# One preln transformer block: the order of fill, projection and VectorE's products in steps 8 to 60

## The chip, the cores and the metric

The kernel runs on one core of one Trainium2 chip. Its time is the device time of one execution, in microseconds (us). The engines are PE (TensorE, matmuls), DVE (VectorE), ACT (ScalarE), POOL (GpSimd) and SP (SyncE, which issues DMA transfers). Each engine executes its own instructions in the order in which they are written, and waits for others by semaphores: an instruction that waits holds all that stands behind it on its engine.

## The reference

```python
x = x + attn(layernorm(x), wq, wk, wv, wo)      # x: 1024 x 256, 16 heads of 128
x = x + ffn(layernorm(x), w1, b1, w2, b2)       # 256 -> 1024 -> 256, exact gelu, ternary weights

def attn(h):
    q, k, v = heads(h @ wq), heads(h @ wk), heads(h @ wv)
    q, k = rotary(q), rotary(k)                 # x1*cos - x2*sin, x2*cos + x1*sin
    s = q @ k.T * 128**-0.5                     # only keys q-127 .. q are valid
    return concat(softmax(s) @ v) @ wo

def ternary(w):                                 # for w1 and w2
    scale = max(mean(abs(w)), 1e-8)
    return clip(round(w / scale), -1, 1)
```

## The kernel before, in words

The attention part is a software pipeline of 64 steps. A step n is one head and one quarter (256 rows) of the sequence: for n below 56, head n // 4 and quarter n % 4; the last eight steps, two heads, are taken in another order. A "chunk" m is half of the sequence of q or k of one head; there are 64 of them too, and a step computes chunk n + 4 ahead. fp32 products are made of three matmuls each, with operands split in a high and a low part (`_hi`, `_lo`).

What one step does, engine by engine, in steps 8 to 60 (`turned_first(n)` is true for these):

- PE: it transposes the probabilities of step n - 1 (`transpose_probs`, L488), computes the scores of step n (`scores`, L477), projects chunk n + 4 (`project`, L423, 512 columns each), then the "fill" (`fill`: either `project_v`, L442, a piece of v, or `project_out`, L459, a piece of the output product, twelve matmuls of 256 columns either way), then weighs v by the probabilities of step n - 1 (`weigh_v`, L505 to L508).
- DVE: it masks the transposed probabilities of step n - 1 (`mask_pt`, L873), selects the valid scores and takes their maximum (`merge`, L856 to L862), makes the low part of the head's output (`ot_lo`, L880), multiplies chunk n + 4 by the sine table (`times_sin`), takes the reciprocal of the row sums (`inverse_sum`, L867), multiplies the chunk by the cosine table (`times_cos`, both L825 or L827), and adds the output piece of the fill of step n - 1 to the residual (`add_out`, L886). In the even steps 34 to 48 one piece of the feed-forward weights is made ternary behind these (`ternary`, L904: two inputs in SBUF).
- ACT: `ot_hi` (L695), the exponentials (`exps`, L676), the copy of v if the fill of step n - 1 was one (`copy_v`, L690), the scaling of the probabilities by the reciprocal (`scale_probs`, L683), and the high part of the rotated chunk n + 3 (`rothi`, L671). Behind it, in some steps, stands the high part of a weight (L654, L660, L666), and in steps 18 to 25 a sum of absolute weights (L700).
- SP: the product by the sine table has its two halves swapped by two DMA transfers (`swap`, L306) as soon as it is there; weights are loaded behind it in the queue.
- POOL: the low part of chunk n + 2 (`rotlo`, L1088), the sum of the cosine product and the swapped sine product of chunk n + 3 (`rotate`, L1083), and, in some steps, the low part of a weight (L1070, L1074, L1078) or the first half of a ternary piece (`below`, L1095, odd steps 33 to 47).

So two chains run from step to step. The probabilities: scores, `merge`, `exps`, `inverse_sum`, `scale_probs`, and then PE's `transpose_probs(n)` at the head of step n + 1. The chunks: `project`, `times_sin`, the swap, `rotate`, `rothi`, `rotlo`, and then the scores of a later step.

"o step" below is a step on whose DVE list an `add_out` stands (n % 8 = 4 to 7); "v step" one on whose ACT list a `copy_v` stands (n % 8 = 0 to 3). Where n % 4 = 1, `weigh_v` has no L507 in it, since the first rows have no earlier keys.

Of the kernel before, what the change touches and what calls it, by code (L numbers as in the profile page):

```python
# [16 lines left out]
def preln_block_kernel(nc, x, wq, wk, wv, wo, w1t, b1, w2t, b2, cos_t, sin_t, in_prev, mask_t, ident, out):  # L17
# [13 lines left out]
    CHUNKS = 4 * HEADS  # L31
# [3 lines left out]
    with ExitStack() as ctx:  # L35
# [147 lines left out]
        LP = STEPS - 8  # L183
# [18 lines left out]
        def fills(n):  # L202

            if n >= LP:
                e = 4 * PAIRS
                return ((("v", e - 3),), (("v", e - 2),), (("v", e - 1),), (("o", e - 8),), (("o", e - 7),),
                        (("o", e - 4), ("o", e - 3)), (("o", e - 6),), (("o", e - 5),))[n - LP]
            if n < 2:
                return (("v", n + 2),)
            p, s = n // 8, n % 8  # L210
            if s == 7:
                return (("v", 4 * p + 4),)
            if s < 3:
                return (("v", 4 * p + s + 1),) if p > 0 else ()
            return (("o", 4 * p + s - 7),) if p > 0 else ()
# [19 lines left out]
        def turned_first(n):  # L235

            return 8 <= n < STEPS - 3
# [134 lines left out]
        def _(pe):  # L372
# [13 lines left out]
            def transpose_half(half):  # L386
                banks = xt_banks[half]
                if half == 0:
                    pe.wait_ge(cos_done, CHUNKS)
                else:  # L390
                    pe.wait_ge(pt_masked, STEPS)
                    pe.wait_ge(otlo_done, STEPS)
                for t in range(4):
                    pe.wait_ge(xn_ready, NT + half * 4 + t + 1)
                    for kd in range(KD):
                        tr = nc.tensor.transpose(banks[kd][:, t * P:(t + 1) * P],
                                                 xnorm[:, half * 4 + t, kd * P:(kd + 1) * P], ident_sb[:])
                        if t == 3:
                            tr.then_inc(xt_ready, 1)
# [11 lines left out]
            def project(m):  # L411
                head, c = chunk(m)
                a = head % 2
                if c == 0:
                    pe.wait_ge(qklo_done, head + 1)
                if m >= 2:
                    pe.wait_ge(cos_done, m - 1)
                if m in (0, 2):
                    pe.wait_ge(xt_lo_done, m + 2)
                n = 0  # L420
                for kd in range(KD):
                    for wt, xt in ((qk_lo[a], xT_hi), (qk_hi[a], xT_lo), (qk_hi[a], xT_hi)):
                        last = mm(PR[m % 2][:], wt[:, c % 2, kd], xt[:, kd, half_of(c)],  # L423
                                  start=(n == 0), stop=(n == 3 * KD - 1))
                        n += 1
                last.then_inc(proj_done, 1)
# [37 lines left out]
            def scores(n):  # L464
                head, j = step(n)
                if j % 2 == 0:
                    pe.wait_ge(rotlo_done, chunk_of[head, j + 1] + 1)
                if n >= 2:
                    pe.wait_ge(exp_done, 2 * n - 2)
                for i in range(2):  # L470
                    t = 2 * j + i
                    k0 = max(t - 1, 0)
                    o0 = i * 256 + (k0 - t + 1) * P
                    terms = ((rot_lo(head, 0), rot_hi(head, 1)), (rot_hi(head, 0), rot_lo(head, 1)),
                             (rot_hi(head, 0), rot_hi(head, 1)))
                    for p_, (q, k) in enumerate(terms):
                        last = mm(SC[n % 2][:, o0:(i + 1) * 256], q[:, t * P:(t + 1) * P], k[:, k0 * P:(t + 1) * P],  # L477
                                  start=(p_ == 0), stop=(p_ == 2))
                last.then_inc(scores_done, 1)

            def transpose_probs(n):
                pe.wait_ge(scaled, n + 1)
                if n > 0:
                    pe.wait_ge(pt_masked, n)
                if n == MEANS_AT:
                    pe.wait_ge(mean_read, 2)
                for i in range(2):
                    last = nc.tensor.transpose(PT[:, i * P:(i + 1) * P], probs[n % 2][:, i], ident_sb[:])  # L488
                last.then_inc(pt_done, 1)
# [20 lines left out]
            def means_of_abs():  # L510
                pe.wait_ge(abs_done, 8)
                pe.wait_ge(pt_masked, MEANS_AT - 1)
                mm(PT[:, 256:264], mean_ones[:], abs_sum[:].rearrange("p k i -> p (k i)"),
                   start=True, stop=True).then_inc(mean_done, 1)

            def fill(n):
                for kind, i in fills(n):
                    (project_v if kind == "v" else project_out)(i)
# [78 lines left out]
            for n in range(3, STEPS):  # L597
                if n == MEANS_AT:
                    means_of_abs()
                if turned_first(n):  # L600
                    transpose_probs(n - 1)
                scores(n)
                if not turned_first(n):
                    transpose_probs(n - 1)
                if n + 4 < CHUNKS:
                    project(n + 4)
                fill(n)
                if n == STEPS - 1:
                    transpose_half(0)
                weigh_v(n - 1)  # L610
# [173 lines left out]
        def _(dve):  # L784
# [30 lines left out]
            def xt_lo_half(half):  # L815
                hs = slice(half * HALF, (half + 1) * HALF)
                for kd in range(KD):
                    dve.wait_ge(xt_hi_done, 4 + half * 2 + kd + 1)
                    tt(xT_lo[:, kd, hs], xt_banks[half][kd][:], xT_hi[:, kd, hs].bitcast(F32),
                       ALU.subtract).then_inc(xt_lo_done, 1)  # L820
# [8 lines left out]
            def times_sin(m):  # L829
                dve.wait_ge(proj_done, m + 1)  # L830
                if m >= 2:
                    dve.wait_ge(rot_done, m - 1)
                times_table(by_sin[m % 2], m, sin_sb).then_inc(sin_done, 1)
# [31 lines left out]
            def inverse_sum(n):  # L865
                dve.wait_ge(exp_done, 2 * n + 2)
                nc.vector.reciprocal(rinv[:, n % 2], rowsum[:, n % 2]).then_inc(rinv_done, 1)  # L867
# [14 lines left out]
            def add_out(w):  # L882
                c = w % 4
                dve.wait_ge(wo_done, o_at[w] + 1)
                ts = slice(2 * c, 2 * c + 2)
                tt(xres[:, ts], VO[w % 2][:].rearrange("p (t d) -> p t d", t=2), xres[:, ts], ALU.add).then_inc(wo_added, 1)  # L886
# [95 lines left out]
            for n in range(3, STEPS):  # L982
                if n == STEPS - 2:
                    add_out(4 * PAIRS - 3)
                    tile_stats(1, 2)
                    tile_stats(1, 3)
                if n >= STEPS - 2:
                    ot_lo(n - 2)
                if n == STEPS - 1:
                    mask_pt(n - 1)  # L990
                if turned_first(n):
                    mask_pt(n - 1)
                if n == MEANS_AT:
                    mean_sums()
                merge(n)
                if not turned_first(n) and n < STEPS - 1:
                    mask_pt(n - 1)
                if n == STEPS - 2:
                    moments(3)
                if n < STEPS - 2:  # L1000
                    ot_lo(n - 2)
                if n + 4 < CHUNKS:
                    times_sin(n + 4)
                if n == STEPS - 1:
                    xt_lo_half(0)
                inverse_sum(n)
                if n == STEPS - 2:
                    add_out(4 * PAIRS - 6)
                    normalise(3)
                if n + 4 < CHUNKS:  # L1010
                    times_cos(n + 4)
                if n <= LP + 4:
                    for kind, w in fills(n - 1):
                        if kind == "o":
                            add_out(w)
                if n == LP + 4:
                    add_out(4 * PAIRS - 7)
                if n == STEPS - 3:
                    add_out(4 * PAIRS - 4)
                    tile_stats(1, 0)  # L1020
                    tile_stats(1, 1)
                if n == MEANS_AT:
                    thresholds()
                i = (n - BELOW_AT - 1) // 2
                if n > BELOW_AT and (n - BELOW_AT) % 2 == 1 and i < PIECES:
                    ternary(i)
# [145 lines left out]
```

## Time and profile before

| what | value |
|---|---|
| median of 3 runs | 346.85 us (346.25 to 346.94) |
| the profiled execution | 346.98 us, of it a span of 345.1 us |
| granted TensorE clock | 1.000 of full speed |
| PE busy | 335.9 us, 97% of the span |
| DVE busy | 272.0 us, 79% |
| POOL busy | 222.1 us, 64% |
| ACT busy | 208.0 us, 60% |
| chain that ended last | PE 85%, DVE 7%, POOL 2% |

Busy time is the union of an engine's instructions. Matmuls overlap in the pipeline, so the distance between two starts, and not the duration shown, is what one of them costs.

### The profile page before, as it was taken

What the parts mean: (1) busy time and instruction counts of PE and PEld (TensorE: products, weight loads), DVE (VectorE), ACT (ScalarE), POOL (GpSimd) and SP (SyncE); (2) the same over time, 40 slices, a digit from 0 to 9 for tenths busy, and PEclk for the clock granted to TensorE, in tenths of its full rate; (3) what the DMA queues carried; (4) which work ended last, traced back from release to release, by engine and by line L of the source; (5) the groups of instructions that cost most, each with busy time, mean ns of one, the idle gap of its engine ahead of it and who ended that gap; (6) DMA issues with size and microseconds to landing.
All of it is one profiled execution on the core that took longest, in us unless ns stands there. A gap on an engine that the chain in (4) does not pass through costs nothing.

```text
span 345.1 us, 6651 instructions
## 1 busy us (share of the span) xinstructions
PE 335.9 (97%) x2270; PEld 307.3 (89%) x2270; DVE 272.0 (79%) x608; ACT 208.0 (60%) x628; POOL 222.1 (64%) x181
## 2 busy tenths in 40 slices
PE   7997999999999999999999999999999999999996
PEld 6975789999999999999999999999999999988986
DVE  5889886778777886688789988898778777887782
ACT  3445766666677677655675566555775665567280
POOL 4326898765867586757899988898777567330400
DMA  7732563455554333333333333333322232000001
GB/s 222 188 109 62 140 167 92 123 142 146 141 147 94 84 91 93 92 92 80 78 84 81 83 89 92 93 92 93 91 64 56 49 83 60 0 3 0 32 30 61
DMA packets 29024, 31.23 MB, mean 90 GB/s; under 512 B 3392, under 2 KB 20288, under 8 KB 28992
## 3 DMA queue, kind: packets, MB, share of 16 engines
q1 hardware_dynamic: 28672, 30.29, 34.5%
q10 hardware_dynamic: 320, 0.52, 0.4%
q8 instruction: 18, 0.29, 0.4%
q14 instruction: 14, 0.11, 0.1%
HBM read 12.98 MB, written 1.05 MB: 41 GB/s over the span
## 4 chain that ended last, share of the span: by engine, by line
PE 85%; DVE 7%; POOL 2%; issue 2%; DMA 2%; ACT 1%; SPq 0%; DVEq 0%; POOLq 0%
PE PR L423 22%; PE VO L459 12%; PE VO L442 12%; PE SC L477 12%; PE OT L505 7%; PE PT L488 4%; PE OT L508 4%; PE OT L507 3%; PE VO L541 2%; PE PR L534 2%; PE SC L534 2%; PE SC L541 1%; POOL turn L1083 1%; DMA xres<-in_x 1%; DMA swapped<-by_sin 1%
## 5 line engine op out<-in xcount | busy, mean ns | idle before, releaser
L1088 POOL TENSOR_TENSOR gT_lo<-turn,gT_hi 128x512 fp32r<-128x512 f32 x61 | 80.6, 1322 | 40.9 <-ACT gT_hi L671 40.3
L1083 POOL TENSOR_TENSOR turn<-turn,swapped 128x512 f32<-128x512 f32 x61 | 78.9, 1293 | 30.7 <-DMA swapped<-by_sin 30.3
L676 ACT ACTIVATE probs<-SC,negmax 128x128 f32<-128x128 f32 x128 | 45.8, 363 | 68.6 <-DVE negmax L862 68.4
L873 DVE TENSOR_TENSOR probsT<-PT,mask_sb 128x512 f32<-128x512 f32 x64 | 44.1, 689 | 39.0 <-PE PT L488 38.8
L683 ACT ACTIVATE probs<-probs,rinv 128x128 f32<-128x128 f32 x128 | 44.4, 394 | 17.0 <-DVE rinv L867 17.0
L423 PE MATMUL PR<-xT_hi,qk_lo 128*128 128x512 f32 x128 | 50.5, 395 | 0.2 <-DVE xT_lo L812 0.2
L423 PE MATMUL PR<-xT_hi,qk_hi 128*128 128x512 f32 x128 | 50.6, 395 | 0.0
L423 PE MATMUL PR<-xT_lo,qk_hi 128*128 128x512 f32 x128 | 50.5, 394 | 0.0
L671 ACT CAST gT_hi<-turn 128x512 fp32r<-128x512 f32 x64 | 38.9, 608 | 10.8 <-POOL turn L1083 8.7
L477 PE MATMUL SC<-gT_hi,gT_lo 128*128 128x256 f32 (+1 forms) x128 | 41.3, 322 | 1.8 <-DVE gT_lo L848 1.8
L459 PE MATMUL VO<-o_lo,gT_hi 128*128 128x256 f32 x128 | 36.2, 283 | 0.3 <-DVE gT_lo L880 0.3
L505 PE MATMUL OT<-probsT,v_sb 128*128 128x256 f32 x120 | 36.0, 381 | 0.5 <-DVE gT_lo L880 0.4
L442 PE MATMUL VO<-v_lo,xT_hi 128*128 128x256 f32 x128 | 36.1, 282 | 0.0
L442 PE MATMUL VO<-v_hi,xT_hi 128*128 128x256 f32 x128 | 36.1, 282 | 0.0
L442 PE MATMUL VO<-v_hi,xT_lo 128*128 128x256 f32 x128 | 36.0, 281 | 0.0
L477 PE MATMUL SC<-gT_lo,gT_hi 128*128 128x256 f32 (+1 forms) x128 | 35.9, 281 | 0.0
L459 PE MATMUL VO<-o_hi,gT_hi 128*128 128x256 f32 x128 | 35.8, 280 | 0.0
L459 PE MATMUL VO<-o_hi,gT_lo 128*128 128x256 f32 x128 | 35.8, 280 | 0.0
L477 PE MATMUL SC<-gT_hi 128*128 128x256 f32 (+1 forms) x128 | 35.7, 279 | 0.0
L862 DVE TENSOR_REDUCE negmax<-SC 128x2 f32<-128x256 f32 x64 | 27.1, 424 | 2.2
L423 PEld LDWEIGHTS PR<-xT_hi,qk_hi 128*128 128x128 f32 x128 | 24.0, 187 | 5.1
L695 ACT CAST gT_hi<-OT 128x256 fp32r<-128x256 f32 x60 | 21.9, 365 | 9.8 <-PE OT L508 9.4
(126 smaller groups left out, 912.0 us busy)
## 6 DMA issues: line engine op xcount, KB each, us to landing
swapped<-by_sin SPq DMA_DIRECT2D x124, 128.0 KB, 2.3
v_raw<-in_wv SPq DMA_DIRECT2D x8, 256.0 KB, 2.9
qk_raw<-in_wq SPq DMA_DIRECT2D x16, 128.0 KB, 2.6
qk_raw<-in_wk SPq DMA_DIRECT2D x16, 128.0 KB, 2.8
o_raw<-in_wo SPq DMA_DIRECT2D x8, 256.0 KB, 3.0
xres<-in_x SPq DMA_DIRECT2D x4, 256.0 KB, 3.7
w_raw<-in_w1t SPq DMA_DIRECT2D x4, 256.0 KB, 3.4
w_raw<-in_w2t SPq DMA_DIRECT2D x4, 256.0 KB, 3.0
```

Of the source, the lines that this page charges most:

```text
L423: last = mm(PR[m % 2][:], wt[:, c % 2, kd], xt[:, kd, half_of(c)], start=(n == 0), stop=(n == 3 * KD - 1))
L442: last = mm(VO[v % 2][:, i * 256:(i + 1) * 256], xt[:, kd, t * P:(t + 1) * P], wt[:, kd], start=(n == 0), stop=(n == 3 * KD - 1))
L459: last = mm(VO[w % 2][:, i * 256:(i + 1) * 256], ot[:, t * P:(t + 1) * P], wt[:, a], start=(n == 0), stop=(n == 5))
L477: last = mm(SC[n % 2][:, o0:(i + 1) * 256], q[:, t * P:(t + 1) * P], k[:, k0 * P:(t + 1) * P], start=(p_ == 0), stop=(p_ == 2))
L505: mm(o[:, 0:2 * P], v_sb[:, t, hs], shared, start=True, stop=False)
L671: copy(rot_hi(head, c % 2)[:, half_of(c)], turn[m % 4][:]).then_inc(rothi_done, 1)
L676: nc.scalar.activation(probs[n % 2][:, i], SC[n % 2][:, i * 256 + P:(i + 1) * 256], ACT.Exp, bias=negmax[:, n % 2, i:i + 1], accum_out=row ...
L683: last = nc.scalar.activation(probs[n % 2][:, i], probs[n % 2][:, i], ACT.Copy, scale=rinv[:, n % 2, i:i + 1])
L862: nc.vector.tensor_reduce(negmax[:, n % 2], sc[:, :, 1], AX.X, ALU.max, negate=True).then_inc(negmax_done, 1)
L873: tt(probsT[:], PT[:, 0:256].rearrange("p (i q) -> p i q", i=2).unsqueeze(2).broadcast_to([P, 2, 2, P]), mask_sb[:].unsqueeze(1).broadcast ...
L1083: tt(turn[m % 4][:], turn[m % 4][:], swapped[m % 2][:], ALU.add).then_inc(rot_done, 1)
L1088: tt(rot_lo(head, c % 2)[:, half_of(c)], turn[m % 4][:], rot_hi(head, c % 2)[:, half_of(c)].bitcast(F32), ALU.subtract).then_inc(rotlo_don ...
```

## The change

In PE's list the fill of steps 8 to 59 stands ahead of the projection of chunk n + 4, and no longer behind it. In DVE's list of the same steps `times_sin` stands behind `inverse_sum`, and `add_out` of the previous step's fill ahead of both, and no longer behind `times_cos`. In step 60 there is no chunk left, so only DVE's `add_out` moves there. No instruction is added or removed, and the lists of ACT, POOL and SP stay as they are.

```diff
@@ tensor engine
-                if n + 4 < CHUNKS:
+                if turned_first(n) and n + 4 < CHUNKS:
+                    fill(n)
                     project(n + 4)
-                fill(n)
+                else:
+                    if n + 4 < CHUNKS:
+                        project(n + 4)
+                    fill(n)
@@ vector engine
-                if n + 4 < CHUNKS:
+                if n + 4 < CHUNKS and not turned_first(n):
                     times_sin(n + 4)
                 if n == STEPS - 1:
                     xt_lo_half(0)
+                if turned_first(n):
+                    for kind, w in fills(n - 1):
+                        if kind == "o":
+                            add_out(w)
                 inverse_sum(n)
+                if n + 4 < CHUNKS and turned_first(n):
+                    times_sin(n + 4)
...
                 if n + 4 < CHUNKS:
                     times_cos(n + 4)
-                if n <= LP + 4:
-                    for kind, w in fills(n - 1):
-                        if kind == "o":
-                            add_out(w)
```

On PE, step 37, from the last matmul of the scores (L477) on; L423 is the projection, L459 the fill, L505 to L508 `weigh_v`. Before:

```order
L477 MATMUL SC<-gT_hi 128x256
L423 MATMUL PR<-xT_hi,qk_lo 128x512
L423 MATMUL PR<-xT_lo,qk_hi 128x512
L423 MATMUL PR<-xT_hi,qk_hi 128x512
L423 MATMUL PR<-xT_hi,qk_lo 128x512
L423 MATMUL PR<-xT_lo,qk_hi 128x512
L423 MATMUL PR<-xT_hi,qk_hi 128x512
L459 MATMUL VO<-o_lo,gT_hi 128x256
L459 MATMUL VO<-o_hi,gT_lo 128x256
```

And now, the end of the same step, from the last matmuls of the fill on:

```order
L459 MATMUL VO<-o_hi,gT_lo 128x256
L459 MATMUL VO<-o_hi,gT_hi 128x256
L423 MATMUL PR<-xT_hi,qk_lo 128x512
L423 MATMUL PR<-xT_lo,qk_hi 128x512
L423 MATMUL PR<-xT_hi,qk_hi 128x512
L423 MATMUL PR<-xT_hi,qk_lo 128x512
L423 MATMUL PR<-xT_lo,qk_hi 128x512
L423 MATMUL PR<-xT_hi,qk_hi 128x512
L505 MATMUL OT<-probsT,v_sb 128x256
```

The projection moved from the place behind the scores to the place ahead of `weigh_v`; all else keeps its place.

On DVE, step 36 from `ot_lo` on, up to the mask of step 37's list. Line numbers behind the change are four higher. Before:

```order
L880 TENSOR_TENSOR gT_lo<-OT,gT_hi 128x256
L825 SCALAR_TENSOR_TENSOR by_sin0<-PR0,sin_sb 128x512
L867 RECIPROCAL rinv<-rowsum 128x2
L825 SCALAR_TENSOR_TENSOR turn0<-PR0,cos_sb 128x512
L886 TENSOR_TENSOR xres<-VO0,xres 128x512
L904 SCALAR_TENSOR_TENSOR w1_sb<-w1_raw,thr,w1_sb 128x512
L873 TENSOR_TENSOR probsT<-PT,mask_sb 128x512
```

And now:

```order
L884 TENSOR_TENSOR gT_lo<-OT,gT_hi 128x256
L890 TENSOR_TENSOR xres<-VO0,xres 128x512
L871 RECIPROCAL rinv<-rowsum 128x2
L829 SCALAR_TENSOR_TENSOR by_sin0<-PR0,sin_sb 128x512
L829 SCALAR_TENSOR_TENSOR turn0<-PR0,cos_sb 128x512
L908 SCALAR_TENSOR_TENSOR w1_sb<-w1_raw,thr,w1_sb 128x512
L877 TENSOR_TENSOR probsT<-PT,mask_sb 128x512
```

The two products by the tables stand next to each other behind the reciprocal, and the ternary piece stands right behind them, ahead of the mask.

## Rows read from the trace of the kernel before

**Rows 1.** Waits of PE, 45 to 300 us: engine, line, releaser, total us, times, longest.

```profile
PE VO L459 <- DVE gT_lo L880: 0.3, 1, 0.3
PE PT L488 <- ACT probs L683: 0.3, 1, 0.3
```

**Rows 2.** Timeline of PE, end of steps 37 and 41: start us, us, line, names, shapes.

```profile
187.26 0.28 PE L459 MATMUL VO<-o_lo,gT_hi 128*128 128x256 f32 x1
...
188.66 0.60 PE L505 MATMUL OT<-probsT,v_sb 128*128 128x256 f32 x2
...
189.32 0.38 PE L488 MATMUL PT<-ident_sb,probs 128*128 128x128 f32 x2
...
207.52 0.38 PE L488 MATMUL PT<-ident_sb,probs 128*128 128x128 f32 x2
```

**Rows 3.** Timeline of PE in a step that has L507.

```profile
157.11 0.38 PE L507 MATMUL OT<-probsT,v_sb 128*128 128x128 f32 x2
157.33 0.39 PE L508 MATMUL OT<-probsT,v_sb 128*128 128x128 f32 x2
```

**Rows 4.** Timeline of DVE, end of step 36 and start of 37.

```profile
182.85 0.69 DVE L825 SCALAR_TENSOR_TENSOR by_sin<-PR,sin_sb 128x512 f32<-128x512 f32 x1
183.46 0.15 DVE L867 RECIPROCAL rinv<-rowsum 128x2 f32<-128x2 f32 x1
183.53 0.67 DVE L825 SCALAR_TENSOR_TENSOR turn<-PR,cos_sb 128x512 f32<-128x512 f32 x1
184.12 0.68 DVE L886 TENSOR_TENSOR xres<-VO,xres 128x512 f32<-128x512 f32 x1
184.72 0.74 DVE L904 SCALAR_TENSOR_TENSOR w_sb<-w_raw,thr,w_sb 128x512 fp32r<-128x512 f32 x1
185.38 0.68 DVE L873 TENSOR_TENSOR probsT<-PT,mask_sb 128x512 f32<-128x512 f32 x1
...
186.88 0.41 DVE L880 TENSOR_TENSOR gT_lo<-OT,gT_hi 128x256 fp32r<-128x256 f32 x1
```

**Rows 5.** Timeline of ACT: scaling of step 36, first exponential of step 37 (o steps).

```profile
183.65 0.69 ACT L683 ACTIVATE probs<-probs,rinv 128x128 f32<-128x128 f32 x2 [0.38 <-DVE rinv L867]
...
187.00 0.37 ACT L676 ACTIVATE probs<-SC,negmax 128x128 f32<-128x128 f32 x1 [1.48 <-DVE negmax L862]
```

**Rows 6.** Timeline of ACT, step 41 (a v step).

```profile
205.19 0.37 ACT L676 ACTIVATE probs<-SC,negmax 128x128 f32<-128x128 f32 x1 [1.48 <-DVE negmax L862]
...
206.45 0.69 ACT L683 ACTIVATE probs<-probs,rinv 128x128 f32<-128x128 f32 x2
```

**Rows 7.** Timeline of DVE: the sine product of chunk 39, in step 35.

```profile
178.29 0.69 DVE L827 TENSOR_TENSOR by_sin<-PR,sin_sb 128x512 f32<-128x512 f32 x1 [0.17 <-PE PR L423]
```

**Rows 8.** Timeline of POOL, step 36: sum of chunk 39, a weight's low part.

```profile
181.94 1.30 POOL L1083 TENSOR_TENSOR turn<-turn,swapped 128x512 f32<-128x512 f32 x1 [0.27 <-DMA swapped<-by_sin]
183.19 1.29 POOL L1074 TENSOR_TENSOR v_lo<-v_raw,v_hi 128x512 fp32r<-128x512 f32 x1
```

**Rows 9.** Timeline of POOL, step 34: a weight's low part.

```profile
174.21 1.29 POOL L1070 TENSOR_TENSOR qk_lo<-qk_raw,qk_hi 128x512 fp32r<-128x512 f32 x1
```

**Rows 10.** Timeline of DVE, step 34: the first ternary piece.

```profile
174.95 1.10 DVE L904 SCALAR_TENSOR_TENSOR w_sb<-w_raw,thr,w_sb 128x512 fp32r<-128x512 f32 x1
```

**Rows 11.** Timeline of ACT, an early step in which PE waits for it.

```profile
29.88 0.69 ACT L683 ACTIVATE probs<-probs,rinv 128x128 f32<-128x128 f32 x2 [1.63 <-DVE rinv L867]
```

**Rows 12.** The same place on PE.

```profile
30.63 0.44 PE L488 MATMUL PT<-ident_sb,probs 128*128 128x128 f32 x2 [0.38 <-ACT probs L683]
```

**Rows 13.** DMA queues, 130.5 to 131.0 us: kind, packets, MB, share of 16 engines.

```profile
q8 instruction: 1, 0.02, 18.2%
```

**Rows 14.** Timeline of POOL: the sum of chunk 28, in step 25.

```profile
133.55 1.28 POOL L1083 TENSOR_TENSOR turn<-turn,swapped 128x512 f32<-128x512 f32 x1 [2.02 <-DMA swapped<-by_sin]
```

**Rows 15.** Timeline of ACT, step 26: scaling, behind a list without gaps.

```profile
138.04 0.70 ACT L683 ACTIVATE probs<-probs,rinv 128x128 f32<-128x128 f32 x2
```

**Rows 16.** Timeline of PE: the transposes of step 26's probabilities.

```profile
139.25 0.38 PE L488 MATMUL PT<-ident_sb,probs 128*128 128x128 f32 x2
```

## The prediction

> **What bounds the kernel now.** I read the share of busy time first (PE 97%, no other engine over 79%), then the waits of PE, then the timelines of PE, DVE, ACT and POOL over two or three steps. Between 45 and 300 us, which holds all the steps that change, PE waits twice, for 0.6 us together [rows 1]. Everywhere else one matmul starts when the one before it lets it. So PE's own work is the time, and the change neither adds nor removes a matmul. It can win 0.6 us at most in these steps, and only if it removes those two waits. What it can lose is set by the slack of the others, so the question is which operand is late for PE behind the change.
>
> The operand with the least slack is the scaled probabilities, which PE transposes at the end of each step. In step 41 the scaling starts at 206.45 and ends 0.69 later, 207.14 [rows 6], and PE takes the result at 207.52 [rows 2]: 0.38 us of slack. Steps with L507 have 0.22 us more, the distance between its start and that of L508 [rows 3].
>
> **PE's part of the change.** The fill takes 188.66 - 187.26 = 1.40 us [rows 2]. The projection now ends 1.40 us later in the step, and `weigh_v` starts when it did: the same matmuls stand between. What waits for the projection moves by 1.40 us: the sine product, the swap (SP has nothing else to do meanwhile, and the weight loads behind the swap move with it), the sum on POOL, its high part on ACT, its low part on POOL. The low part is wanted by scores three steps later; adding up the timelines of POOL and PE I find 1.8 to 3.2 us of slack there in most steps, so that 1.40 us fits. The fill's own readers (copy of v, `add_out`) get their data earlier, and had not been late: nothing.
>
> **DVE's part, a plain step.** Before, sine, reciprocal, cosine and `add_out` stand at 182.85, 183.46, 183.53 and 184.12, the ternary piece at 184.72 [rows 4]. Spacings: 0.61, 0.07, 0.59, 0.60. Now `add_out` and the reciprocal come before the sine product, in time that DVE would spend waiting for the projection; sine and cosine come last. The sine product starts 1.40 us later, at 184.25 for the step of these rows, the cosine at 184.86 and what stands behind it at 185.45. The mask of the next step stood at 185.38 [rows 4]. In a step without a ternary piece it is therefore late by 0.1 us (0.3 where the step before has no L507). That passes to the exponentials, and less of it to the reciprocal, which no longer stands behind the sine. With 0.38 us or more of slack, the plain steps cost nothing. That is the cover, and it is thin: 0.3 us more on DVE would break it.
>
> **DVE's part, the eight ternary steps.** In the even steps 34 to 48 the ternary piece stands between the cosine and the next mask. Before, it lay in DVE's idle time and the mask was on time. Now it begins at 185.45. POOL at that time: the sum of chunk 39 started 181.94 - 178.29 = 3.65 us behind its sine product [rows 7, 8]; the sine product is now at 179.69, the sum at 183.34, it takes 1.25, and the low part of the weight runs from 184.59 to 185.88. Where a ternary piece started while such a POOL instruction ran, it ended only 0.55 us behind that instruction's end (174.95 + 1.10 = 176.05 against 174.21 + 1.29 = 175.50) [rows 9, 10]. I take the same here: its end is 186.43, the mask starts 0.08 before (as 185.38 to 184.72 + 0.74), at 186.35. That is 0.97 us late. All eight have such a POOL instruction behind the sum, since the weights' low parts fall in even steps.
>
> Odd step, o kind (37): the exponentials follow the mask by 187.00 - 185.38 = 1.62 [rows 4, 5], now 187.97. On DVE `ot_lo` follows the mask by 1.50, at 187.85, `add_out` at about 188.22 and the reciprocal 0.60 later at 188.82, when the sums are just there. Scaling follows the reciprocal by 183.65 - 183.46 = 0.19 and takes 0.69: its end is 189.70. PE takes it 0.06 later, as where it waited before (30.63 against 29.88 + 0.69) [rows 11, 12]: 189.76, where it was 189.32. PE waits 0.44 us; in an o step with L507 (39, 47) 0.22.
>
> Odd step, v kind (41): exponentials at 205.19 + 0.97 = 206.16, the scaling 1.26 later as before (the copy of v stands between) at 207.42, its end at 208.11, PE at 208.17 in place of 207.52. PE waits 0.65; with L507 (35, 43) 0.43.
>
> Sum: two each of 0.44, 0.22, 0.65 and 0.43, together 3.5 us. Every one of them is PE's idle time, and nothing gives it back, since each following step is again bound by PE. Bounds: if the ternary piece does not collide with POOL it takes 0.74, the mask is late by 0.73, and the eight waits sum to 1.6. If the sum of the chunk is itself late on POOL under the ternary piece (a wait for DMA like the 2.02 of [rows 14] in place of 0.27), the piece ends at about 186.9, 0.5 us later; with that in four of the eight steps the sum is 5.4.
>
> **Late transfers.** Now and then a swap lands late: POOL waited 2.02 us for chunk 28 [rows 14], and five more waits are of 1.6 to 2.3 us. One packet of 0.02 MB of instructions was under way in that swap's flight [rows 13]. Before, this reached ACT and mostly stopped there. Step 26 is the tightest: ACT's list ran without a gap from the late chunk to the scaling at 138.04 [rows 15]. 1.40 us later its end is 138.04 + 0.70 + 1.40 = 140.14, with 0.06 at PE 140.20, against 139.25 [rows 16]: PE would wait 0.95. But the fetch follows PE's instructions and not the swap, and the swap is now 1.40 us later against it. So it may miss the swap here and meet another one. Ends: nothing, if no late swap meets a full ACT list; 2.5 us, if step 26 pays in full and steps 15, 16, 18 and 61 pay half a microsecond or less each. I take 0.8, near step 26's own.
>
> The Trainium skill (Runtime: NRT & Kernel Launch, section on instruction fetch mechanics) says that a sequencer fetches 16 KiB blocks through its own DMA queue and that this is mostly hidden. The size agrees with this row of the trace; for "hidden" the 2.02 us of wait beside it speaks against. By that rule the term of the late transfers would be nothing and the execution 350.5.
>
> **Sum.** 346.98 us is the profiled execution. 346.98 + 3.5 + 0.8 = 351.3. The profile lies 0.13 above the median of the runs, so I state 351.2 for the median.
>
> **Rivals.**
> - *The collision does not bite, only the delay of transfers and half of the ternary term remain.* The ternary piece, if it starts uncontended, costs 1.6 us, and the transfers 0.3: 348.8. For it: the piece at 184.72 took only 0.74 us, its POOL instruction having ended at 184.48 [rows 4, 8]. Against: in all eight POOL is now in the middle of an instruction by the sum above.
> - *Not slower: the earlier reciprocal absorbs the ternary piece.* Place: ACT between exponentials and scaling. The sine product no longer stands ahead of the reciprocal, which in an o step could follow the exponentials by 0.83 us in place of 1.07 and so win 0.24; if the mask could be late by 0.6 us without delaying `merge` (that is, if the scores were what `merge` waits for and DVE caught up), PE would never wait and the time would be 346.9; with the two waits of [rows 1] gone, 346.3. It decides at a mask 0.6 us late in an o step; I find 0.97. In v steps the copy of v fills the same gap, so nothing is won there. Against it too: mask and `merge` follow each other without a gap in these rows.
> - *Worse: low parts on POOL come late for the scores.* In step 15 I find 1.84 us of slack before, 0.45 behind the change. A swap late by another 1 us there, or in the steps 36 to 48 where POOL is fullest, stops PE for 0.5 to 1 us each: with two or three of these and the upper bound of the ternary term, 354.
> - *The change does not do what it says.* The lists show that it does, so I give this nothing.
>
> **Chances.** The forecast (349.6 to 353): 0.67. The milder one (347.6 to 349.6): 0.14. Worse (over 353): 0.08. Within 0.2% of before: 0.08. Faster: 0.03. 0.2%, or 0.7 us, is about what a measurement of this kernel tells from no change. Slower than that is therefore 0.89. Range: 348.2 to 353.2.
>
> **What would show it.** Right: PE's waits list L488 for ACT's scaling with some eight waits of 0.2 to 0.7 us, in the odd steps 35 to 49; DVE's mask in these steps starts 1.1 to 1.4 us behind the scores' start and not 0.3; the step after a plain one keeps its length of 4.4 to 4.6 us; DVE's wait for the projection grows and its wait ahead of the mask nearly vanishes. Wrong: waits of PE at L488 in plain steps (then the plain steps' cover is gone, and the loss is larger than 5 us), waits at L477 (the low parts), or no wait at all in steps 35 to 49 with the mask late (then ACT had slack that I did not see).

## The result, and the profile after

| | before | changed |
|---|---|---|
| median | 346.58 us (4 runs, 346.25 to 346.94) | 351.45 us (4 runs, 351.12 to 351.80) |
| profiled execution | 346.98, span 345.1 | 351.23, span 349.4 |

The ratio is 1.0122, with a 95% interval of 1.0081 to 1.0162. In a later session the changed kernel was timed again: 1.0132 (1.0117 to 1.0146), 351.35 us; one execution of 1009 us of that session is left out, with its profile. The prediction said 351.2, 348.2 to 353.2.

The waits of PE between 45 and 300 us, which answer to [rows 1]:

```profile
PE PT L488 <- ACT probs L687: 1.1, 4, 0.5
PE VO L459 <- DVE gT_lo L884: 0.9, 1, 0.9
PE OT L505 <- DVE gT_lo L884: 0.8, 3, 0.3
```

The waits at L488 are there, for ACT's scaling, but this list counts an idle time only behind the modelled end of the last matmul: it adds up to 2.8 us where 5 are lost. The distance from one step's first scores matmul to the next is the better measure. Against the kernel before, the steps of the changed kernel are longer by (us; the length up to the start of the step named):

| stretch | before to changed | where |
|---|---|---|
| steps 9 to 35 | +0.25 | about 0.01 in each |
| steps 36 to 50 | +3.84 | 36: 0.47, 38: 1.20, 40: 1.02, 42: 0.30, 44: 0.14, 46: 0.19, 48: 0.08, 50: 0.34 |
| steps 51 to 60 | +0.09 | about 0.01 in each |
| steps 61 to 63 | +0.83 | 61: 0.21, 62: 0.63 |

Together 5.00 us. The prologue of this execution was 0.65 us shorter (step 8 began at 52.42 us in place of 53.07; in the profiles of e1 to e8 it began between 52.4 and 54.1), so the span grew by 4.3 us only.

What happens on DVE around the end of step 36, to be read beside [rows 4]:

```profile
184.32 0.69 DVE L829 SCALAR_TENSOR_TENSOR by_sin<-PR,sin_sb 128x512 f32<-128x512 f32 x1 [0.79 <-PE PR L423]
184.93 0.68 DVE L829 SCALAR_TENSOR_TENSOR turn<-PR,cos_sb 128x512 f32<-128x512 f32 x1
185.53 1.78 DVE L908 SCALAR_TENSOR_TENSOR w_sb<-w_raw,thr,w_sb 128x512 fp32r<-128x512 f32 x1
187.23 0.68 DVE L877 TENSOR_TENSOR probsT<-PT,mask_sb 128x512 f32<-128x512 f32 x1
...
188.62 0.42 DVE L884 TENSOR_TENSOR gT_lo<-OT,gT_hi 128x256 fp32r<-128x256 f32 x1
```

On POOL at the same time (for [rows 8]):

```profile
184.23 1.28 POOL L1080 TENSOR_TENSOR v_lo<-v_raw,v_hi 128x512 fp32r<-128x512 f32 x1
185.47 1.29 POOL L1094 TENSOR_TENSOR gT_lo<-turn,gT_hi 128x512 fp32r<-128x512 f32 x1
```

And on ACT and PE (for [rows 5] and [rows 2]):

```profile
188.74 0.37 ACT L680 ACTIVATE probs<-SC,negmax 128x128 f32<-128x128 f32 x1 [3.17 <-DVE negmax L866]
...
189.78 0.69 ACT L687 ACTIVATE probs<-probs,rinv 128x128 f32<-128x128 f32 x2 [0.23 <-DVE rinv L871]
```

```profile
189.19 0.67 PE L505 MATMUL OT<-probsT,v_sb 128*128 128x256 f32 x2 [0.28 <-DVE gT_lo L884]
...
190.53 0.44 PE L488 MATMUL PT<-ident_sb,probs 128*128 128x128 f32 x2 [0.45 <-ACT probs L687]
```

The chain of the prediction is all there: the sine product waits 0.79 us for the projection, the ternary piece stands behind the cosine product, the mask comes 2.09 us behind the start of the step's scores (185.14) in place of 0.30, exponentials and scaling follow, and PE waits. But this piece takes 1.78 us. It began at 185.53, at the changeover from POOL's low part of a weight to POOL's low part of the chunk (185.47 to 186.76), and ended 187.31, 0.55 us behind the end of the second. That makes `ot_lo` so late too that PE waits for it at L505, which the prediction did not have.

Over the eight pieces, each ended 0.54 to 0.63 us behind the end of a POOL instruction. What differs is which. The third and the fourth:

```profile
195.72 1.85 DVE L908 SCALAR_TENSOR_TENSOR w_sb<-w_raw,thr,w_sb 128x512 fp32r<-128x512 f32 x1
...
205.98 0.74 DVE L908 SCALAR_TENSOR_TENSOR w_sb<-w_raw,thr,w_sb 128x512 fp32r<-128x512 f32 x1
```

```profile
195.74 1.29 POOL L1094 TENSOR_TENSOR gT_lo<-turn,gT_hi 128x512 fp32r<-128x512 f32 x1
...
206.06 1.82 POOL L1094 TENSOR_TENSOR gT_lo<-turn,gT_hi 128x512 fp32r<-128x512 f32 x1
```

At 195.72 the piece began 0.02 us ahead of POOL's instruction and was held through it; at 205.98 it was 0.08 ahead, took 0.74, and POOL's instruction was stretched to 1.82 us instead. The pieces of steps 36 and 38 lost and were held through a whole POOL instruction. The piece of step 34 met the last 0.58 us of one and took 1.13 us; the five others met at most the last 0.36 us and took 0.74 to 0.91 us.

The last steps, on POOL, ACT and PE:

```profile
297.08 1.28 POOL L1089 TENSOR_TENSOR turn<-turn,swapped 128x512 f32<-128x512 f32 x1 [1.97 <-DMA swapped<-by_sin]
```

```profile
298.39 0.62 ACT L675 CAST gT_hi<-turn 128x512 fp32r<-128x512 f32 x1 [1.66 <-POOL turn L1089]
298.92 0.36 ACT L699 CAST gT_hi<-OT 128x256 fp32r<-128x256 f32 x1
```

```profile
295.44 0.67 PE L505 MATMUL OT<-probsT,v_sb 128*128 128x256 f32 x2 [0.20 <-DVE gT_lo L884]
...
299.80 0.39 PE L459 MATMUL VO<-o_lo,gT_hi 128*128 128x256 f32 x1 [0.88 <-DVE gT_lo L884]
```

The swap of the last chunk landed late, POOL's sum was at 297.08, ACT's high part of the chunk held the head's output (L699) to 298.92, DVE's low part of it followed, and PE, whose fill of step 61 needs it, waited 0.88 us where it had waited 0.3 [rows 1].

DVE's two waits that the prediction named as a sign changed as it said. Its wait ahead of the mask nearly vanished and its wait for the projection grew. Before, 45 to 300 us (total us, times, longest):

```profile
DVE probsT L873 <- PE PT L488: 38.0, 48, 1.3
...
DVE by_sin L827 <- PE PR L423: 4.6, 27, 0.3
DVE by_sin L825 <- PE PR L423: 1.8, 11, 0.2
```

Changed:

```profile
DVE by_sin L829 <- PE PR L423: 19.2, 26, 0.9
DVE by_sin L831 <- PE PR L423: 16.7, 23, 0.9
...
DVE probsT L877 <- PE PT L488: 1.4, 2, 1.2
```

### The profile page after: what moved, and what is told of

The parts are those of the page before. It is cut to its first block, busy times and chain, and to the rows that moved or that the text cites. A ratio compares the mean times of both kernels' runs of the same rounds, so it can differ in the third digit from the quotient of the medians.

```text
span 349.4 us, 6651 instructions
## 1 busy us (share of the span) xinstructions
PE 338.1 (97%) x2270; PEld 307.6 (88%) x2270; DVE 269.4 (77%) x608; ACT 209.3 (60%) x628; POOL 222.2 (64%) x181
## 3 DMA queue, kind: packets, MB, share of 16 engines
HBM read 12.98 MB, written 1.05 MB: 40 GB/s over the span
## 4 chain that ended last, share of the span: by engine, by line
PE 74%; DVE 12%; ACT 4%; POOL 4%; issue 3%; DMA 2%; SPq 1%; DVEq 0%; POOLq 0%
PE PR L423 20%; PE VO L442 11%; PE VO L459 10%; PE SC L477 10%; PE OT L505 6%; PE PT L488 4%; PE OT L508 3%; PE VO L541 2%; PE SC L534 2%; PE OT L507 2%; POOL turn L1089 2%; DVE w_sb L908 2%; PE PR L534 2%; POOL gT_lo L1094 1%; DVE probsT L877 1%
## 5 line engine op out<-in xcount | busy, mean ns | idle before, releaser
L1094 POOL TENSOR_TENSOR gT_lo<-turn,gT_hi 128x512 fp32r<-128x512 f32 x61 | 81.9, 1342 | 19.5 <-ACT gT_hi L675 19.5
L675 ACT CAST gT_hi<-turn 128x512 fp32r<-128x512 f32 x64 | 39.7, 620 | 29.6 <-POOL turn L1089 27.4
L423 PE MATMUL PR<-xT_hi,qk_lo 128*128 128x512 f32 x128 | 51.1, 399 | 0.2 <-DVE xT_lo L816 0.2
L423 PE MATMUL PR<-xT_lo,qk_hi 128*128 128x512 f32 x128 | 50.4, 394 | 0.0
L423 PE MATMUL PR<-xT_hi,qk_hi 128*128 128x512 f32 x128 | 50.2, 392 | 0.0
L477 PE MATMUL SC<-gT_hi,gT_lo 128*128 128x256 f32 (+1 forms) x128 | 41.3, 323 | 1.8 <-DVE gT_lo L852 1.8
L829 DVE SCALAR_TENSOR_TENSOR by_sin<-PR,sin_sb 128x512 f32<-128x512 f32 x32 | 22.1, 690 | 20.2 <-PE PR L423 20.2
L505 PE MATMUL OT<-probsT,v_sb 128*128 128x256 f32 x120 | 36.0, 381 | 1.3 <-DVE gT_lo L884 1.3
L459 PE MATMUL VO<-o_lo,gT_hi 128*128 128x256 f32 x128 | 36.3, 284 | 0.9 <-DVE gT_lo L884 0.9
L477 PE MATMUL SC<-gT_hi 128*128 128x256 f32 (+1 forms) x128 | 35.9, 281 | 0.0
L477 PE MATMUL SC<-gT_lo,gT_hi 128*128 128x256 f32 (+1 forms) x128 | 35.9, 280 | 0.0
L459 PE MATMUL VO<-o_hi,gT_lo 128*128 128x256 f32 x128 | 35.8, 280 | 0.0
L459 PE MATMUL VO<-o_hi,gT_hi 128*128 128x256 f32 x128 | 35.8, 280 | 0.0
L831 DVE TENSOR_TENSOR by_sin<-PR,sin_sb 128x512 f32<-128x512 f32 x32 | 22.1, 690 | 16.9 <-PE PR L423 16.7
```

Of the source, the lines that this page charges most:

```text
L459: last = mm(VO[w % 2][:, i * 256:(i + 1) * 256], ot[:, t * P:(t + 1) * P], wt[:, a], start=(n == 0), stop=(n == 5))
L505: mm(o[:, 0:2 * P], v_sb[:, t, hs], shared, start=True, stop=False)
L675: copy(rot_hi(head, c % 2)[:, half_of(c)], turn[m % 4][:]).then_inc(rothi_done, 1)
L1094: tt(rot_lo(head, c % 2)[:, half_of(c)], turn[m % 4][:], rot_hi(head, c % 2)[:, half_of(c)].bitcast(F32), ALU.subtract).then_inc(rotlo_don ...
```

## The experiments

All steps 8 to 60 are meant where nothing else is said. "Lengths" are step lengths against the kernel before, from each profile, as in the table above.

**e1: the ternary piece earlier.**

```diff
                 if n < STEPS - 2:
                     ot_lo(n - 2)
+                if piece_here:            # even steps 34 to 48
+                    ternary(i)
...
                 inverse_sum(n)
+                # in these steps add_out stands here
                 if n + 4 < CHUNKS and turned_first(n):
                     times_sin(n + 4)
...
-                    ternary(i)            # behind times_cos
```

> The changed kernel with the ternary piece of the even steps 34 to 48 moved on VectorE from behind the cosine product to right behind the low part of the head's output; in these steps the output sum stands behind the reciprocal, ahead of the sine product. Theory A (the ternary piece between cosine product and next mask makes the mask late, and eight masks cost 3.7 us of PE): steps 35 to 50 go back to the lengths of before (steps 36, 38 and 40 to 4.60, 4.38 and 4.63 us from 5.07, 5.58 and 5.65); the whole is 3.7 us faster than the changed kernel, 347.8 us. Theory B (POOL's load in steps 33 to 48 and late transfers are what stops PE, the piece only shows it): under 1 us is won, 350.6 us or more.

Measured: 347.87 us (9 runs), ratio to before 1.0028 (1.0014 to 1.0042). Steps 36 to 50 lose 0.34 us in place of 3.84, steps 61 to 63 lose 0.21. In step 36 the piece now runs while DVE would wait for ACT or PE:

```profile
183.02 0.74 DVE L908 SCALAR_TENSOR_TENSOR w_sb<-w_raw,thr,w_sb 128x512 fp32r<-128x512 f32 x1
183.68 0.16 DVE L871 RECIPROCAL rinv<-rowsum 128x2 f32<-128x2 f32 x1
183.75 0.67 DVE L890 TENSOR_TENSOR xres<-VO,xres 128x512 f32<-128x512 f32 x1
184.59 0.69 DVE L829 SCALAR_TENSOR_TENSOR by_sin<-PR,sin_sb 128x512 f32<-128x512 f32 x1 [0.16 <-PE PR L423]
```

The sine product waits for PE again, so the piece costs nothing in this step. In one step it did: the piece of step 38 met a POOL instruction, took 1.44 us and held the reciprocal behind it, and that step is 0.24 us longer, most of the 0.34. Theory A holds, B falls: POOL had the same work. The place of this one instruction in eight steps carries 3.5 us of the loss.

**e2: the piece in the gap ahead of the sine product.**

```diff
                 inverse_sum(n)
+                if piece_here:
+                    ternary(i)
                 if n + 4 < CHUNKS and turned_first(n):
                     times_sin(n + 4)
```

> The changed kernel with the ternary piece between the reciprocal and the sine product, where VectorE waits 0.8 us for the projection and the piece alone needs 0.74. Theory A with the collision (a piece that begins while a POOL instruction runs ends 0.55 us behind that instruction's end): POOL's sum of the chunk runs from 2.8 to 4.1 us of the step, the piece starts at about 2.9 to 3.0, so it ends at 4.6 where it meets the sum, and the sine product is 0.75 us late; of the 3.7 us only part is won, 349 to 351 us. Theory C (the piece costs its 0.74 us wherever it stands, collisions matter little): the gap hides it all, 347.8 us.

Measured: 349.31 us (6 runs), 1.0069 (1.0050 to 1.0087). Steps 36 to 50 lose 1.67 us, step 23 loses 0.34 and step 62 0.29. The gap is 0.8 us wide and the piece needs 0.74, but it falls on POOL's sum of the chunk:

```profile
183.66 0.17 DVE L871 RECIPROCAL rinv<-rowsum 128x2 f32<-128x2 f32 x1
183.74 1.77 DVE L908 SCALAR_TENSOR_TENSOR w_sb<-w_raw,thr,w_sb 128x512 fp32r<-128x512 f32 x1
185.44 0.68 DVE L829 SCALAR_TENSOR_TENSOR by_sin<-PR,sin_sb 128x512 f32<-128x512 f32 x1
```

```profile
183.67 1.30 POOL L1089 TENSOR_TENSOR turn<-turn,swapped 128x512 f32<-128x512 f32 x1
184.91 1.76 POOL L1080 TENSOR_TENSOR v_lo<-v_raw,v_hi 128x512 fp32r<-128x512 f32 x1
```

It began 0.07 us behind the sum and ended 0.54 behind the sum's end. Five of the eight pieces took 1.77 to 1.83 us. So theory C, by which the gap hides the piece, falls.

**e3: POOL's low parts of the weights one step later**, DVE's list as in the changed kernel.

```diff
-                if s == 2 and 0 < p < PAIRS - 1:
-                    qklo(2 * p + 2)       # and so on: vlo, qklo, olo
+                w = n - 1 if 34 <= n - 1 < 49 else n
+                if not 34 <= n < 50 or n % 2:
+                    ...                   # the same four, for step w
```

> The changed kernel with POOL's low parts of the weights moved, in the even steps 34 to 48, by one step (behind the chunk's sum of the odd step that follows, ahead of the ternary threshold there). VectorE's list stays. Theory A with the collision: no low part of a weight runs when the ternary piece begins at 4.9 us of the step; the chunk's sum, later now since POOL's odd steps are fuller, ends about then. Pieces should take 0.74 to 0.9 us and end earlier; none is held through two POOL instructions (1.78 and 1.85 us before); the loss in steps 35 to 50 falls from 3.7 to about 1.6 us, total 349.3 us. Theory C (the piece's length is its own): nothing changes, 351.4 us. Theory B (POOL's load stops PE): PE waits at the scores for low parts in odd steps, total over 351.4.

Measured: 349.21 us (6 runs), 1.0068 (1.0054 to 1.0083). Seven of the eight pieces took 0.74 us and one 0.95, although nothing on DVE was changed; steps 36 to 50 lose 1.42 us, near the 1.6 that the prediction gave for pieces without a collision. So of the 3.84 us nearly two thirds are the collision, and the rest is what pieces of 0.74 us cost by their place. Theories B and C fall. Two stalls of 0.15 and 0.26 us in steps 23 and 27 of this profile are not due to the edit; they come and go between profiles.

**e4: PE's part alone.** `fill(n)` ahead of `project(n + 4)`, DVE's list as before.

> The kernel before with only PE's part of the change: fill ahead of projection in steps 8 to 59, VectorE's list as before. The sine product, 1.40 us later, then holds the reciprocal: from 2.99 us of the step to 3.80 + 0.61 = 4.41, scaling ends at 5.29, and PE wants the result at 4.24 to 4.5. Theory A: every one of the 52 steps is 0.8 to 1.1 us longer, about 50 us in all, 397 us. Theory D (VectorE's reordering is incidental, PE's order is what costs): near 351.4 us.

Measured: 398.84 us (5 runs), 1.1508 (1.1486 to 1.1530). Each step is 0.92 to 1.18 us longer but for step 28 (0.78), and PE waits at L488 54 times, 40.3 us. In an early step:

```profile
62.20 0.69 DVE L831 TENSOR_TENSOR by_sin<-PR,sin_sb 128x512 f32<-128x512 f32 x1 [1.59 <-PE PR L423]
62.81 0.15 DVE L871 RECIPROCAL rinv<-rowsum 128x2 f32<-128x2 f32 x1
```

The reciprocal, a thing of 0.15 us that was ready, stands behind a wait of 1.59. Theory D falls: DVE's reordering is what makes the late projection bearable.

**e5: VectorE's part alone.** PE's list as before.

> The kernel before with only VectorE's part of the change: output sum, reciprocal, sine product, cosine product; PE's projection stays ahead of the fill. Theory A (the loss comes from the projection being late, which puts sine and cosine product at the end of the step): the sine product waits for the reciprocal and not for PE, starts at about 2.9 us of the step in place of 2.4, the cosine product is over at 4.1, the next mask is on time at 0.3, the ternary piece ends by 4.9: within 0.3 us of the kernel before, 346.8 us. Theory E (the order on VectorE is bad in itself): the eight steps 36 to 50 show waits as in the changed kernel, over 348 us.

Measured: 347.63 us (12 runs, 346.56 to 349.53), 1.0029 (1.0012 to 1.0045). Not quite what was expected: 0.9 us slower. Steps 36 to 50 lose 0.40 and no others lose in a row; steps 23 and 55 lose 0.15 and 0.09. The pieces took 0.78 to 1.89 us here too: each met a POOL instruction, the sum of a chunk or the low part of a weight. So the mask was late here as well, by up to 0.95 us, which theory A had not foreseen. The longest piece:

```profile
212.54 1.89 DVE L904 SCALAR_TENSOR_TENSOR w_sb<-w_raw,thr,w_sb 128x512 fp32r<-128x512 f32 x1
214.36 0.68 DVE L873 TENSOR_TENSOR probsT<-PT,mask_sb 128x512 f32<-128x512 f32 x1
```

```profile
212.59 1.29 POOL L1072 TENSOR_TENSOR qk_lo<-qk_raw,qk_hi 128x512 fp32r<-128x512 f32 x1
```

It was 0.05 us ahead of POOL and lost. This costs PE little because a piece begins 4.04 to 4.09 us behind the start of its step's scores, where in the changed kernel it begins 4.95 to 5.02 us behind: the same collision ends about 0.9 us earlier. A mask that is late all the same costs as much as there: 0.61 us late in step 41 it cost 0.12 us, 0.95 us late in step 43 it cost 0.26. Of its 0.9 us the profile shows 0.6 between steps 8 and 63; the spread of its runs is wide, and I cannot say more of the rest. Theory E falls in size: 0.4 us in these steps, not 3.8.

**e6: the piece early and the order of before from step 57 on.** As e1, and `late_projection(n) = turned_first(n) and n < 57` in the conditions of the change.

> The changed kernel with the ternary piece behind the low part of the output (as in the first experiment) and with the order of before on PE and VectorE from step 57 on. Theory A: steps 36 to 50 as in the first experiment, and steps 61 and 62 as before (0.2 us less than there, 0.8 less than in the changed kernel): 347.5 us, still not under the kernel before, since PE has nothing to win. Rival: the loss in steps 61 and 62 comes from the chain of chunks as a whole and stays: 347.9.

Measured: 347.67 us (12 runs), 1.0035 (1.0018 to 1.0052). Steps 61 to 63 lose nothing now, steps 36 to 50 lose 0.30 (0.19 of it in step 38 again, whose piece took 1.40 us), steps 9 to 35 0.25. It is the best version with the late projection, no faster than e1 within the error, and no version beats the kernel before.

**e7: the change in steps 34 to 49 alone.** `late_projection(n) = turned_first(n) and 34 <= n < 50`.

> The kernel before with the change in steps 34 to 49 alone. Theory A: the whole loss of the ternary steps is there, steps 36 to 50 are about 3.7 us longer in sum, all others as before: 350.4 us. Theory F (the loss in these steps needs the lag that 25 earlier steps build up in POOL and ACT): under 2 us, 348.7 us or less.

Measured: 351.09 us (6 runs, 350.21 to 355.31), 1.0152 (1.0112 to 1.0192). Steps 9 to 35 are as before (+0.01), steps 36 to 50 lose 5.62 us in the profiled execution, one of its longer ones (353.6 us). There the pieces of steps 36, 38 and 48 were held (1.77, 1.87 and 1.91 us). Steps 36, 38 and 40 to 44 are longer by 0.54, 1.20, 1.04, 0.30 and 0.15, nearly the changed kernel's numbers. Step 46 is longer by 0.61 in place of 0.19: a late swap put POOL's sum of a chunk beside the piece, the case that the prediction had as its upper bound. Step 50, behind the third held piece, is longer by 1.47 in place of 0.34. The third held piece on DVE, then POOL's late sum for step 46 and the instruction that held the piece:

```profile
245.25 1.91 DVE L912 SCALAR_TENSOR_TENSOR w_sb<-w_raw,thr,w_sb 128x512 fp32r<-128x512 f32 x1
```

```profile
225.53 1.29 POOL L1097 TENSOR_TENSOR turn<-turn,swapped 128x512 f32<-128x512 f32 x1 [2.21 <-DMA swapped<-by_sin]
...
245.31 1.30 POOL L1102 TENSOR_TENSOR gT_lo<-turn,gT_hi 128x512 fp32r<-128x512 f32 x1
```

Theory F falls: the loss needs no lag from earlier steps. The ternary loss has no fixed size: no piece was held in e3, two were in the changed kernel, three here.

**e8: the piece with one SBUF input.**

```diff
-                nc.vector.scalar_tensor_tensor(dest, raw, thr[...], dest.bitcast(F32), ALU.is_gt, ALU.subtract)
+                nc.vector.tensor_scalar(dest, raw, thr[...], None, ALU.is_gt)
```

> The changed kernel with the ternary piece in its place, but as a tensor_scalar that reads one SBUF tensor (weights above the threshold) in place of two; the subtraction of the weights below the threshold is left out. Theory G (two SBUF inputs make an instruction collide with POOL): no piece is held, each takes about 0.7 us or less, the masks are late by 0.7 us at most and never by 1.8, steps 36 to 50 lose 1.6 us or less, 349.2 us or less. Theory H (any SBUF-to-SBUF instruction of VectorE collides): some pieces again take 1.1 to 1.8 us, ending about 0.5 us behind the end of a POOL instruction, and the time is near the changed kernel's.

This kernel leaves out the subtraction, so its feed-forward weights are not those of the reference; it serves only to time the piece. Measured: 350.47 us (6 runs, 348.10 to 351.70), 1.0118 (1.0095 to 1.0141); the profiled execution is the shortest of them, and in it steps 36 to 50 lose 0.84 us. The pieces took 0.48 to 0.92 us. The first, and POOL beside it:

```profile
175.90 0.85 DVE L908 TENSOR_SCALAR w_sb<-w_raw,thr 128x512 fp32r<-128x512 f32 x1
```

```profile
175.17 1.29 POOL L1075 TENSOR_TENSOR qk_lo<-qk_raw,qk_hi 128x512 fp32r<-128x512 f32 x1
176.43 1.48 POOL L1093 TENSOR_TENSOR gT_lo<-turn,gT_hi 128x512 fp32r<-128x512 f32 x1
```

It ended 0.29 us behind the end of the POOL instruction and stretched the next one to 1.48, so an instruction with one SBUF input collides too; theory G falls in that. All eight pieces met a POOL instruction and ended 0.28 to 0.33 us behind its end, where the piece with two inputs ended 0.55 behind it; that is, the shorter piece (0.48 us where it hardly meets POOL) is held to the end of POOL's instruction like the longer one. No piece was held through a whole instruction in this profile, but its other executions were up to 3.6 us longer and nothing shows why. So this experiment does not settle the time: the median lies between what G and H said.

**e9: the changed kernel once more.**

> The changed kernel once more, for a narrower interval and for whether the held pieces fall on the same steps. Every theory: 351.4 us within 0.4. If the profile again has the pieces of steps 36 and 38 held through two POOL instructions, the place is set by the program's order; if others are held, it is a matter of some tens of nanoseconds.

Measured: 351.35 us (3 runs). Whether the held pieces fall on the same steps was not seen: the profiled execution is the one of 1009 us, in which PE's projection matmuls took 1.00 us each in place of 0.40, for a reason that nothing here shows, and no piece met a POOL instruction. e7, another kernel with the same order in these steps, had the pieces of steps 36 and 38 held again and a third besides.

## Why the prediction was right

**What bounds.** PE, and every wait added to it is lost: between steps 8 and 63 the sum of the longer steps is the whole difference. Right. I had 0.6 us as the most that could be won; nothing was won in any version.

**PE's part.** The shift by 1.40 us: the sine product began at 3.80 us of the step in place of 2.38, that is 1.42 later. The scores never waited for a low part, as forecast. Not foreseen: 0.01 us in each step, 0.34 in sum over the steps 9 to 35 and 51 to 60. It goes with PE's new order: e5, with the old one, does not have it outside its few stalls, nor does e7 in the steps that keep the old one. No wait makes it up. In steps 9 to 33 the matmuls of the projection start 231.6 ns apart in place of 230.4, and those of the fill 118.3 in place of 117.8. Why they do is not shown.

**Plain steps.** The mask 0.1 us late (0.39 against 0.28), 0.3 where forecast (0.62); PE's list has no wait between 48.31 us, ahead of the steps that change, and 180.38, the end of step 35. Right, and e4 shows what the cover was worth.

**Ternary steps.** The mechanism is shown by e1 (place) and e3 (collision). The sum was 3.5, and the eight measured terms below add up to 3.74 (3.84 with the 0.01 of the steps between); but they were not right one by one:

| step of the piece | 34 | 36 | 38 | 40 | 42 | 44 | 46 | 48 |
|---|---|---|---|---|---|---|---|---|
| forecast loss | 0.43 | 0.44 | 0.22 | 0.65 | 0.43 | 0.44 | 0.22 | 0.65 |
| measured | 0.47 | 1.20 | 1.02 | 0.30 | 0.14 | 0.19 | 0.08 | 0.34 |

I let every piece begin in the middle of POOL's low part of a weight. Only the first did (0.71 us into it), and there the forecast was good. The seven others began near its end, since the step with a wait is longer behind its sine product, so that POOL, which follows the sine product, is ahead by as much in the next. Five of them got through sooner than I said: together they lost 1.05 us where the forecast has 2.39. The two that lost were held through the whole next instruction, a case that the prediction did not have (its upper bound has a late sum of the chunk, as in e7): 2.22 us where it has 0.66. The errors cancelled, so that the sum was right is luck, and e7, with a third piece held, lost 5.6 us. The cover was a little larger than I said, too. In step 41 the mask was 0.77 us late, but the exponentials only 0.64 (2.56 against 1.92 us into the step) and the scaling 0.55 (3.73 against 3.18).

**Late transfers.** I took 0.8, near what step 26 would lose. Step 26 lost nothing: chunk 28 was late on POOL as before, but by 1.0 us less (4.41 us behind its sine product in place of 5.40), and its scaling was over 0.18 us before PE took it. The fetch did not move with the swap, as the prediction had it. Before, the block of instructions started 1.39 us behind the issue of that swap's second transfer, which took 4.10 us to land; now it started 0.03 us ahead of it, and the transfer took 3.11. In the trace of the kernel before, six transfers of swaps took 3.7 to 4.4 us, where the median is 2.3, and each had such a block in its flight. That the block is the cause is likely by this, but no experiment tested it. The 0.83 us were lost at the end: 0.63 in step 62 behind the late swap of chunk 63, which the upper end named, and 0.21 in step 61, which no term had. There the step has no projection, `weigh_v` follows the fill at once, and `ot_lo`, 0.2 us later behind the late mask, is the last operand (the row at 295.44). It is the same 0.21 in e1 and in e2 and gone in e6, so it is a fixed cost of the change, while the 0.63 is not (nothing in e1, 0.29 in e2). The term's size was right in this profile and its place wrong, and other profiles with the late projection in all steps lose 0.21 (e1), 0.24 (e3), 0.50 (e2) and 0.58 us (e8) there: luck again.

**The total.** 5.0 us in the steps, and 4.9 between the medians, where the prediction summed to 4.3. That the profiled execution came within 0.1 us of the forecast owes something to its short prologue. That the time is slower, by which path and in which steps was understood beforehand; that the number fits to 0.3 us in the median is in part luck. Of the other signs, waits at L488 in eight odd steps, PE's list shows three (180.38, 190.53 and 200.79 us); the other five are too short for it, and only the step lengths show them. The mask of these steps started 1.05 to 2.16 us behind the scores, where 1.1 to 1.4 was forecast.

**The rivals.** The milder one's condition, pieces that do not collide, is what e3 makes: 349.21, where the rival said 348.8. The one that was not slower needed a mask at most 0.6 us late; it was 0.8 to 1.9.

## What to carry to other kernels

When instructions are moved later on an engine, ask what stands between them and the next deadline in the few steps that differ from the rest: the plain steps cost 0.3 us, eight with one more instruction 3.8. Put work without a deadline where the engine waits anyway and where it does not meet an instruction of another engine that holds it: the eight pieces cost 0.3 us in one gap (e1) and 1.7 us in another (e2). A late producer is bearable only if nothing that is ready stands behind the wait for it (e4).

## What was not expected of the hardware

VectorE's ternary piece and POOL's large instructions (128x512, SBUF to SBUF) take turns by whole instructions. The piece, 0.74 us by itself (fp32, two inputs in SBUF), ended 0.54 to 0.55 us behind the end of a POOL instruction that held it. A piece that won kept its 0.74 us, and POOL's instruction took up to 1.83 us in place of 1.29. A few hundredths of a microsecond in its start decided between 0.74 and 1.9 us: 0.02, 0.05 and 0.06 us ahead of POOL's start it lost (195.72, 212.54 in e5, 245.25 in e7), 0.05 and 0.08 ahead it won (176.77 in e3, 205.98). The two groups meet at 0.05 to 0.06, so the recorded starts alone do not tell the winner there. The winning case of e3, on DVE and POOL:

```profile
176.77 0.74 DVE L908 SCALAR_TENSOR_TENSOR w_sb<-w_raw,thr,w_sb 128x512 fp32r<-128x512 f32 x1
```

```profile
176.82 1.83 POOL L1094 TENSOR_TENSOR gT_lo<-turn,gT_hi 128x512 fp32r<-128x512 f32 x1 [0.73 <-ACT gT_hi L675]
```

This does not hold for all of VectorE's work. In the changed kernel the mask, which has one input in PSUM, took 0.68 to 0.69 us in the 59 cases beside a POOL instruction and in the 5 others, and the small reciprocal (128x2, SBUF to SBUF) took 0.15 to 0.17 us either way. Which operands and sizes collide was tested with the piece alone (e8).
